# A new table of slots, one product for the two 64-row ends of the shared expert, and layers and experts in one block

## The reference

```python
x = x + _L0_attn_ref(_layernorm(x), ...)   # softmax attention of x with itself, two vectors scale it
x = x + _L0_ffn_ref(_layernorm(x), ...)    # 256x256 product of values rounded to e4m3, result bf16
x = x + _L1_attn_ref(_layernorm(x), ...)   # a selective scan (Mamba), below
x = x + _L1_ffn_ref(_layernorm(x), ...)    # 8 experts of which a token takes 2, and a shared one

# L1_attn: layernorm, xc,z = split(xn @ in_proj), causal 4-tap conv, u = silu(xc)
B, C = split(u @ x_proj);  delta = softplus(u @ dt_proj);  A = -exp(A_log)     # 512 channels, 16 states
h = exp(delta * A) * h + (delta * u) * B          # per token, 512 x 16 states
y = (sum over states of h * C + u * D) * silu(z); out = y @ out_proj

# L1_ffn
w = softmax(x @ gate.T) kept for the two best experts
out = sum over experts of w * (silu(x @ g_e.T) * (x @ u_e.T)) @ d_e.T          # inner width 352
shared = (silu(x @ shared_gate.T) * (x @ shared_up.T)) @ shared_down.T         # inner width 704
out = out + sigmoid(x @ shared_expert_gate.T) * shared
```

## Time and profile before

| | |
|---|---|
| median of 3 runs | 3368.53 us (3368.17 to 3368.85) |
| the profiled execution | 3364.8 us, its span 3362.8 us |
| busy: PE, DVE, ACT, POOL | 84%, 76%, 61%, 77% of the span |
| first scan starts, last scan starts | 149.8 us, 2692.0 us |
| one batch in the middle (from scan 0 to the next scan 0) | 162.1 to 163.4 us |
| first expert product starts | 2771.05 us |

### The profile page before, as it was taken

The page is one execution under the profiler, slowest core; times in us unless marked ns, Lnnn a source line. Parts: engine busy times, 40 slices in busy tenths (PEclk is TensorE's granted clock), DMA queues, the critical chain, the costliest instruction groups (busy, mean ns, idle before and its releaser), DMA issues. The chain is left out here.

```text
span 3362.8 us, 46770 instructions
## 1 busy us (share of the span) xinstructions
PE 2834.9 (84%) x12696; PEld 1870.1 (56%) x12697; DVE 2546.5 (76%) x4108; ACT 2064.1 (61%) x3786; POOL 2592.0 (77%) x2474
## 2 busy tenths in 40 slices
PE   3686979797979797888888888888887779999998
PEld 2444555555555555555555555565545447777776
DVE  3498989899989989898999898989897842222222
ACT  3576677676767676766767676767665514444443
POOL 1399898989889898989898989898999913444444
PEclk7897989898989898989999999999998889999999
DMA  2001111111111111111110101010112313333333
GB/s 75 23 32 32 36 44 36 43 39 39 39 39 41 38 39 40 46 33 46 34 51 26 51 29 51 29 48 31 43 36 82 101 56 58 63 63 63 62 62 52
DMA packets 113898, 155.37 MB, mean 46 GB/s; under 512 B 15472, under 2 KB 73264, under 8 KB 113712
## 3 DMA queue, kind: packets, MB, share of 16 engines
q1 hardware_dynamic: 77344, 109.32, 10.4%
q0 software_dynamic: 25728, 34.75, 6.4%
q10 hardware_dynamic: 10640, 9.09, 0.8%
HBM read 107.36 MB, written 45.76 MB: 46 GB/s over the span
## 5 line engine op out<-in xcount | busy, mean ns | idle before, releaser
L872 POOL TENSOR_TENSOR dbu<-du,bbc 128x512 f32<-128x512 f32 x1024 | 1294.2, 1279 | 74.5 <-DVE h L1440 67.8
L1440 DVE TENSOR_TENSOR_SCAN h<-bank,dbu 128x512 f32<-128x512 f32 x1024 | 1227.3, 1212 | 158.7 <-ACT bank L1082 101.9
L1082 ACT ACTIVATE bank<-region,amat 128x512 f32<-128x512 f32 x1024 | 703.6, 691 | 313.3 <-DVE h L1440 299.0
L665 PE MATMUL bank<-ident,h 128*128 128x128 f32 x4096 | 624.9, 289 | 259.5 <-DVE acc L1430 231.4
L665 PEld LDWEIGHTS bank<-ident,h 128*128 128x128 f32 x4096 | 495.6, 148 | 544.3 <-DVE acc L1430 224.7
L858 POOL TENSOR_TENSOR acc<-acc,hTc 128x512 f32<-128x512 f32 x480 | 609.6, 1271 | 103.7 <-ACT hTc L1066 102.1
L1607 POOL DMA_INDIRECT out<-ye,ids x136 | 213.3, 1569 | 347.1 <-DMA out<-ye,ids 311.3
L1066 ACT ACTIVATE hTc<-bank,cT 128x512 f32<-128x512 f32 x480 | 327.3, 682 | 236.6 <-PE bank L665 236.5
L1430 DVE SCALAR_TENSOR_TENSOR acc<-bank,cT,acc 128x512 f32<-128x512 f32 x544 | 395.0, 730 | 38.9 <-PE bank L665 33.4
L619 PE MATMUL bank<-x4T,w_su 128*128 128x512 f32 (+1 forms) x768 | 389.2, 610 | 10.7 <-DVE score L1305 10.7
L1643 DVE SCALAR_TENSOR_TENSOR gg<-gt,bank 128x352 f32<-128x352 f32 x136 | 70.7, 520 | 382.2 <-ACT gt L1577 382.2
(11 more groups left out here) (204 smaller groups left out, 4361.1 us busy)
## 6 DMA issues: line engine op xcount, KB each, us to landing
bbc<-b_scratch SPq DMA_DIRECT2D x256, 256.0 KB, 3.1
xe<-slots_in SPq DMA_DIRECT2D x136, 129.0 KB
region<-in_x SPq DMA_DIRECT2D x16, 512.0 KB, 3.8
out<-x ACTq DMA_DIRECT2D x16, 512.0 KB, 3.1
region<-in_e_gu SPq DMA_DIRECT2D x8, 704.0 KB, 5.4
out<-ye,ids POOLq DMA_INDIRECT x136
slots_in<-dbu SPq DMA_DIRECT2D x16, 129.0 KB, 3.2
slots_in<-x,pos POOLq DMA_INDIRECT x128
```

Source lines behind the costliest of these rows:

```text
L665: last = tr(scan[f"hT{s}.{t}"][:, m * P:(m + 1) * P], h[:, s % 2, m, t * P:(t + 1) * P], ident[:, :])
L872: g.tensor_tensor(dbu[:, n % 4, :], du[:, m, :], bbc[:, (b * NS + s) % NROW, :], ALU.mult).then_inc(S("dbu_ready"), 1)
L1082: f(db(n)[:, :], delta[:, 1 - par, m, :], ACT.Exp, scale=amat[:, m, s:s + 1]).then_inc(S("da_ready"), 1)
L1440: v.tensor_tensor_scan(h[:, s % 2, m, :], db(n)[:, :], dbu[:, n % 4, :], 0.0, ALU.mult, ALU.add)\
```

## The change

1. The table `AT` has new numbers almost throughout. No step is added to it or taken from it. The diff shows two of its twelve lines.
2. Of the six chunks of the shared expert's gate and up products, the last had 64 rows each and a product of its own each (two halves of the contraction each). Their columns now stand side by side in `w_su`, and one product of 128 rows makes both: gate in partitions 0 to 63 of the bank, up in 64 to 127. `up_of` reads the second half of that bank. The loads of `w_su` become four instead of two.
3. `experts` becomes `expert_programs`, which is called inside `layers` and returns one program for each engine. Every engine runs it right behind its own last step. The barrier and the clearing of semaphores are gone, and the waits that stood at the end of the block are divided: SP waits for the padding, the routed rows and the tables, PE for the weights, the tables and the last sum, POOL for the tables and the last store. The experts' tiles lie in memory of `u`, `du` and `bbc`.

```diff
 AT = dict(
-    yT=(0, 0, 1, 2), y=(0, 0, 1, 1), uD=(2, 3, 3, 3), acc0=(1, 2, 2, 2), out=(4, 6), x3=(7, 10), stats5=12, rstd5=11, x4=14,
+    yT=(0, 0, 0, 0), y=(0, 0, 0, 0), uD=(0, 0, 2, 2), acc0=(0, 0, 1, 2), out=(3, 6), x3=(5, 9), stats5=11, rstd5=12, x4=14,
 ...
-    stats3=2, rstd3=1, res=3, r4=4, r4T_pe=5, r4T=3, in_x=(8, 10, 15, 17), ...
+    stats3=0, rstd3=0, res=4, r4=4, r4T_pe=5, r4T=1, in_x=(7, 10, 14, 18), ...
 ...
+FULL = SI // P * P
 for n in range(len(SC)):
-    late.add(f"g{n}", 1, AT["gate"][n], ("sgate_ready", n))
-    late.add(f"u{n}", 1, AT["up"][n], ("su_ready", n))
+    if n < len(SC) - 1:
+        late.add(f"g{n}", 1, AT["gate"][n], ("sgate_ready", n))
+        late.add(f"u{n}", 1, AT["up"][n], ("su_ready", n))
+    else:
+        late.add(f"g{n}", 1, AT["up"][n], ("su_ready", n))
 ...
 def hidden_of(n, name, half):
     at, size = SC[n]
+    if n == len(SC) - 1 and half == 1:
+        return
 ...
-        last = mm(late[f"{name}{n}", b][0:size, :], w_su[:, c, half * SI + at:half * SI + at + size], x4T[:, c, :],
+        first, rows = (half * FULL + at, size) if n < len(SC) - 1 else (2 * FULL, 2 * size)
+        last = mm(late[f"{name}{n}", b][0:rows, :], w_su[:, c, first:first + rows], x4T[:, c, :],
                   start=c == 0, stop=c == DC - 1)
 ...
 def up_of(n):
     size = SC[n][1]
-    late.filled(dve, f"u{n}", b)
     done(dve, "sgate_ready", b, n)
-    v.tensor_tensor(shh[0:size, n, :], late[f"u{n}", b][0:size, :], shh[0:size, n, :], ALU.mult).then_inc(S("su_ready"), 1)
+    if n == len(SC) - 1:
+        up = late[f"g{n}", b][size:2 * size, :]
+    else:
+        late.filled(dve, f"u{n}", b)
+        up = late[f"u{n}", b][0:size, :]
+    v.tensor_tensor(shh[0:size, n, :], up, shh[0:size, n, :], ALU.mult).then_inc(S("su_ready"), 1)
 ...
-nc.clear_and_free_semaphores(taken)
-nc.all_engine_barrier()
-experts(nc, sem, out, ident, banks, xs_d, region, eidi, rowi, fencei)
 ... (PE, behind its turns)
+pe.wait_ge(ew_loaded, 16 * 3 * E)
+pe.wait_ge(table_ready, 3)
+done(pe, "fin_ready", NB - 1)
+expert_pe(pe)
 ... (SP)
-sp_.wait_ge(ew_loaded, 16 * 3 * E)
+done(sp_, "acc_init", NB - 1)
+done(sp_, "du_ready", NB - 1)
 sp_.wait_ge(tails_in, 16 * E)
 sp_.wait_ge(pads_in, 16 * E)
-sp_.wait_ge(S("out_stored"), 16 * (NB + 1))
+sp_.wait_ge(table_ready, 3)
+for w in range(2):
+    sp_.wait_ge(dispatched[w], 16 * TT * NB)
+expert_sp(sp_)
 ... (POOL)
-for w in range(2):
-    pool.wait_ge(dispatched[w], 16 * TT * NB)
+pool.wait_ge(table_ready, 3)
+pool.wait_ge(S("out_stored"), 16 * (NB + 1))
+expert_pool(pool)
```

More of the change, by code:

```diff
@@ L311, in layers @@
-            stats3=2, rstd3=1, res=3, r4=4, r4T_pe=5, r4T=3, in_x=(8, 10, 15, 17), tap=(11, 12, 17, 19), conv=(13, 15, 19, 21),
-            tanh=(13, 15, 20, 21), u=(16, 17, 23, 24), base=12, xBC_pe=24, bs=25, cT_pe=29, cT=31, in_z=(31, 38, 45, 51),
-            z=(33, 40, 48, 53), zs=(38, 43, 50, 55), dt_pe=(26, 34, 40, 49), raw=(30, 38, 44, 52), sp_exp=(32, 44, 49, 55), sp_ln=51,
-            delta=(54, 55, 56, 56), stats1=4, rstd1=4, xn=8, xT=(9, 11), xl=(11, 12), scores=(15, 19, 21, 26), maxs=(18, 21, 25, 29),
@@ new lines, in layers @@
+            ranks=(40, 41, 45, 46, 50, 50, 52, 53), g_pe=(20, 26, 30, 42, 47, 53), g=(22, 27, 32, 43, 50, 54),
+            gate=(24, 29, 34, 46, 53, 56), u_pe=(23, 25, 34, 46, 46, 55), up=(25, 29, 36, 49, 54, 56), d_pe=(51, 56), fin=(57, 63),
+            stats3=0, rstd3=0, res=4, r4=4, r4T_pe=5, r4T=1, in_x=(7, 10, 14, 18), tap=(10, 12, 17, 19), conv=(13, 15, 19, 21),
+            tanh=(13, 15, 21, 21), u=(16, 18, 22, 24), base=16, xBC_pe=24, bs=25, cT_pe=31, cT=35, in_z=(31, 37, 43, 49),
+            z=(33, 40, 46, 53), zs=(38, 43, 48, 55), dt_pe=(26, 33, 38, 49), raw=(30, 37, 44, 53), sp_exp=(33, 43, 49, 55), sp_ln=47,
@@ L1091, in _ @@
             store(NB - 1)
+            expert_act(act)
         @block.vector
```

336 lines of the change are left out of this document (167 added, 169 removed).

## The result

The changed kernel takes 3378.4 us (median of 7 runs, 3377.6 to 3387.1), the kernel before 3368.8 us (7 runs) beside it: a ratio of 1.0032, 95% interval 1.0021 to 1.0044. It is slower, and outside the predicted range of 3290 to 3364 us. The profiled spans are 3376.7 and 3362.8 us, 13.9 us apart; that difference is worked through here.

A forecast was written before the change was run, and what follows sets the result against it. DVE and POOL with their waits were taken to bound a batch, PE the experts' loop. Places summing to 1.7 us less 0.3 gave 1.4 us a batch, 20 us over 14; plus 10.9, 31 us: 3336 us, range 3290 to 3364.

The forecast's parts named there:

- The knots: In each batch: new waits made by the new order, taken off the summed gains as 0.3 us.
- My bound of 11 us: In each batch: the most a new order of steps could gain, from four groups of DVE's waits, 11.1 us.
- the new order does nothing: Rival for the batches: gains become new waits at the next place, DVE's idle time stays; 3355 us, chance 0.18.
- Start of the batch: First `y` to scan 6: later scan 0 is paid from a 3.50 us stall; gain 0.7 us a batch.
- the sliding start: Rival at a batch's start: ACT's `r4`, `res`, `r4T` begin 4.1 us later; 3395 us, chance 0.12.
- Middle: Mid-batch: a 1.12 us wait for ACT shrinks, gain 0.3 us; a 1.18 us wait for a state's transpose stays, gain 0.
- Shared product: Merged gate and up product saves PE 1.8 us a batch: 0.2 us counts there, 1.7 us after the last scan.
- End of the batch: Before scan 60: down products fill PE's 2.00 us idle time, transposes come earlier; gain 0.5 us a batch.
- Seam: Between layers and experts: earlier load 7.3 us, faster clock 1.9 us, merged product 1.7 us; gain 10.9 us.
- The clock as a rival: Rival: TensorE, with less work, runs 16 more records a batch at the halved clock, losing 2.0 us; 3365 us, chance 0.05.

The follow-up runs named there:

- block_only: The kernel before with layers and experts in one block, its slot table and two separate products kept: 3362.4 us, ratio 0.9983.
- product_same_order: The changed kernel with the slot table of the kernel before, TensorE passing the missing product's slots (yield 1.5): 3361.9 us, ratio 0.9982.
- old_new_routing: `product_same_order` with the change's new slots for x4, the router and the places of the tokens only: 3340.9 us, ratio 0.9918.
- routing_two_products: `old_new_routing` with the 64-row ends of gate and up as two products again: 3351.9 us, ratio 0.9956.

## Why the prediction was wrong, step by step

- **The knots, -0.3 us a batch: the step that failed.** I went through the places where before waits, priced what the new table does there, added it up (1.7 us) and took a round 0.3 us off for new waits. A batch got 1.2 us longer instead of 1.4 us shorter, and the last one 5.2 us longer. The new waits a batch are 2.1 us at units 20 and 21, 0.8 more at 29, 0.8 at 36, 1.4 at 45, 1.3 ahead of the rounding at 56, 1.4 at 61, and 2.3 for `y`'s transposes and ahead of scans 2 and 3. They outweigh the ones removed: idle time went from 15.1 to 15.9 us. That the table does it is shown (16.5 us between kernels with one block and the merged product); which slots do is open, with the attention's first half or its meeting with the others as what is left. My bound of 11 us had also left out waits that were there: 22 us in the twelve batches, among them 10.2 us for the scores, which became 15.3. By its mechanism the rival "the new order does nothing" (0.18) fits best, and its time was still 23 us too fast. The clock's 3365 us was nearer in number by luck, since the clock of a batch hardly changed (0.94 and 0.93).
- **Start of the batch, +0.7.** The mechanism was as told: 18.1 us to scan 6, the `x3` ahead of it, `r4` 12.1 us behind the first `y` (so the sliding start did not happen). Setting these slots back, with all others new, changes 1.7 us in all, within the intervals: the term is 0 in this company. The 1.0 us of waiting for `y`'s transposes that I had counted in was 0.77 us; the 1.5 us before scans 2 and 3 I had not.
- **Middle, +0.3 and 0.** The wait of 1.12 us for ACT is 0.8 us: right. That of 1.18 us went, better than told. The new waits in between were not looked for.
- **Shared product, 0.2 a batch.** 704 records, as told, and the read across partitions costs nothing: L1386 on 64 rows takes 0.69 us. Its worth is no property of the product: about 0 in the old order, 0.8 us a batch in the best (11 us over 14 batches), both with the down products a unit later. The 1.7 us behind the last scan did not come: the last gate and up products there are 20 records in 8.83 us instead of 24 in 10.69, but PE then waits 1.7 us longer for the last hidden tile, and the down products behind take 1.5 us longer. That the down products follow it in the slot list I did not see; with the old table this alone would have cost 112 us.
- **End of the batch, +0.5.** The wait before scan 60 is gone and PE's for L494 fell from 2.00 to 1.23 us, as told. (The 1.61 us of the earlier trace rows are not every batch's: four of the twelve have them, with the clock at 1.2 GHz between scans 58 and 60, and the other eight 0.2 us.) What I had named as the risk, ACT late with the scale of the rounding, came: 14.3 us over twelve batches, 1.2 a batch, more than the whole term.
- **Seam, 10.9.** It is 8.7 us. PE's idle time fell by 8.4 us where I had 7.3, with the transposes 1.70 us after PE's last product; the clock's share (1.9 us) failed, since the first tile takes 4.16 us and not 2.63: PE had waited 1.70 and 1.43 us at the seam, and its clock fell to 1.2 GHz at 2785.06 for 3.4 us, as it had at 2767.99 behind the wait of 2.61 us for the last hidden tile. The product's 1.7 us failed as said. The one block alone gives 5 us in the runs.
- **The clock as a rival (0.05).** I had told it for the start of a batch, at 2.0 us; that did not come. As a mechanism it was underrated: at the end of a batch the gap and the slower clock behind it take 0.6 us a batch of the product's gain by unit 58.

In sum: +22.6 us up to the last scan where I had -20 us, and -8.7 us behind it where I had -10.9: 13.9 us slower in the profiled runs and 9.6 us in the medians.

## What to carry to other kernels

When an instruction is taken out of an engine's list, look first at what moves forward into its place, and whether that waits for something late: here one missing step cost 112 us, and one line that passes its slots gave it back. Don't sum the waits that a new order removes; the same trace can't show the ones it makes, and here each group of slots was worth something else in other company (routing: -21 us alone, nothing within the new table). So change one group at a time and keep what pays: old table, one block, merged product and the new routing slots give 3340.9 us, 0.8% under the kernel before and 1.1% under the change.

## What the runs showed of the hardware that was not expected

Taking 1.8 us of products from TensorE in the middle of a batch, and writing what follows a unit later, lowered its granted clock from 1.00 to 0.62 in the stretch behind (batch 6 of `block_only` and `product_same_order`), and records of down products started 0.43 us apart instead of 0.21. The place of such a gap mattered too: with it ahead of the down products scan 60 waited 0.7 us (`old_new_routing`), with it ahead of the rounding's transposes 1.7 us (`routing_two_products`).

With one and the same list of instructions the clock can fall in some batches and not in others: between scans 58 and 60 of the kernel before it does so in 4 of 12 batches, and scan 60 waits 1.6 us in these and 0.2 us in the others.
